# Edge attention: the quotient on another engine, the finish at another place, and twice the scatter buffers

## The chip, the cores and the metric

One core of a Trainium2 chip. The metric is the device time of one execution in microseconds (us). The kernel before took 1922.77 us, the median of three runs (1921.35 to 1923.86).

## The reference, cut to what matters

Two graph layers act on x (50,000 nodes of 64 channels) with 25,000 edges sorted by dst. The first is a pair of spline convolutions with a maximum over the edges of each target. The second, which the change is mostly about, is an attention whose softmax runs over the edges of each target node, channel by channel:

```python
d = gelu(layer_norm(gelu(layer_norm(coords @ Wd1 + bd1)) @ Wd2 + bd2))
logits = w1[target] - w2[source] + d
e = exp(logits - segment_max(logits, target)[target])
denom = segment_sum(e, target)
a = e / denom[target]
out = segment_sum(a * (w3[source] + d), target)
x = x + out
```

Here w1, w2 and w3 are products of relu(layer_norm(x)) with three 64x64 weights.

## The kernel before, in words

All edges are cut into 49 groups (`G`) of 512 (`EG`), four tiles (`TPG`) of 128. Five stages follow one another: preparation and the coordinate network's first part (to about 155 us), convolution 1 (to about 670 us), the network's second part and convolution 2 (to about 1280 us), a last norm and gelu of the network, and the attention (from about 1310 us).

Each engine has its own instruction stream, written out by hand as a function `step(g)` that the helper `each` (L322) calls for every group, four groups to a loop round. The order inside `step` is the order on the engine. Between engines there are only semaphores: `wait(eng, steps, g, name)` waits until the named step of group g is done, and `wait_fill` until a buffer of several has been filled by its DMA. Where a buffer has two copies it is chosen by `g.parity`, where it has four by `g.slot(SLOTS)`.

The attention of group g, with 64 channels of q and k logits and of values stacked in 128 partitions:

- GpSimd (POOL, L637 to L652) gathers the edge sources of group g+3 from `M2` (four indirect DMAs, L584), then scatters the finished rows of group g-1 into the output (four indirect DMAs, L591). The gather needs `gidx` of ScalarE (L828). The scatter needs `sidx` of ScalarE (L855) and the row of VectorE (L1592).
- SyncE loads the running maxima (L536), the cuts between targets (L539) and the base rows `b2` (L546) some groups ahead.
- VectorE (DVE): `normalise` (L1542) makes XT; `x1_ends` (L1532, L1535) adds gathered and loaded rows of group g+1 into `x1`; `running_max` (L1551, and a scan, L1554); `above_held` (L1561); `hold_full` (a scan for group g+2, L1523); `weigh_values` (L1568); `running_sums` (a scan, L1575). For group g-1, `reciprocal` (L1584) inverts the denominators and `finish` multiplies (L1589) and adds the node's own row into `srow` (L1592).
- ScalarE (ACT, L851 to L883): copies indices (L855, L828), copies the turned rows of group g+1 out of PSUM (L860), takes four activations for the two exponentials of group g (L866 to L871), squares (L876), and forms the inverse root of the variance of group g+1 by Ln and Exp (L881, L883).
- TensorE (PE): the q and v products of group g (L1085, two matmuls' worth of passes each), the turn of `x1` of g+1 (L1095), the offsets from d (L1078), the centring (L1099), the variance (L1104), a turn of the maxima of g+2 (L1111), and the turn of the sums of g (L1119) into bank 6, where `output` reads denominators and numerators.

The order of VectorE in the attention is this (L1596):

```python
if (g - 1).within(G): reciprocal(g - 1)
if now:               normalise(g)
if (g - 1).within(G): finish(g - 1)
if (g + 1).within(G): x1_ends(g + 1)
if now:               running_max(g); above_held(g)
if (g + 2).within(G): hold_full(g + 2)
if now:               weigh_values(g); running_sums(g)
```

`srow` and `sidx` (rows and indices to be scattered) have two copies, as have `x1` and the semaphores `scattered`. Convolution 1 scatters through the same two buffers into `T1` (its own `sidx` L765, `srow` L767 and L807); convolution 2 uses `srow` for rows that SyncE stores.

Of the kernel before, what the change touches and what calls it, by code (L numbers as in the profile page):

```python
# [31 lines left out]
P = 128  # L32
# [85 lines left out]
def build(nc, a, out):  # L118
# [17 lines left out]
    with ExitStack() as ctx:  # L136
# [6 lines left out]
        def pair(name):  # L143
            return [sem(name + "_even"), sem(name + "_odd")]
# [128 lines left out]
        full = [att_mem.take([C, EG]) for _ in (0, 1)]  # L273
        XR, rstd = (att_mem.take([P, EG]) for _ in (0, 1))
        pp, d0, rise = (att_mem.take([P, EG]) for _ in range(3))
        held = [att_mem.take([P, EG + 1]) for _ in (0, 1)]
        sums = [att_mem.take([P, EG]) for _ in (0, 1)]
        rec = att_mem.take([P, TPG, C])
        XT = [att_mem.take([P, EG]) for _ in (0, 1)]
        mx3 = [att_mem.take([P, MT * C]) for _ in (0, 1)]  # L280
        squares = lnq.rearrange("p t c -> p (t c)")


# [14 lines left out]

        bank = [ctx.enter_context(nc.psum_tensor(f"bank{i}", [P, 512], F32)) for i in range(8)]


        s_mem = sem("memsets")
        s_rows = sem("rows_loaded")
# [55 lines left out]
        def conv_sems(n):  # L359
            s = {  # L360
                "nload": pair(f"c{n}_nload"), "nstore": pair(f"c{n}_nstore"), "cut": pair(f"c{n}_cut"),
                "z": steps(f"c{n}_z", "z0 z1 z2 z3"), "turn": steps(f"c{n}_turn", "t0 t1 t2 t3"), "prod": steps(f"c{n}_prod", "m0 m1 m2 m3"),
                "zt": steps(f"c{n}_zt", "zt0 zt1 zt2 zt3"), "comb": steps(f"c{n}_comb", "v0 v1 v2 v3 pair quad msg"),
                "npe": steps(f"c{n}_npe", "nt nr"), "out": steps(f"c{n}_out", "out" if n == 1 else "acc out"),
                **signals(f"c{n}", "mt agg at row xn nts"),
            }
            if n == 1:
                s.update(signals("c1", "gidx sidx rowid esum ecen esq evar nsum ncen nsq nvar root a0r"))
                s["gathered"], s["scattered"] = pair("c1_gathered"), pair("c1_scattered")
# [11 lines left out]
        at = {  # L381
            "gathered": [sem(f"a_gathered_{i}") for i in range(SLOTS)], "scattered": pair("a_scattered"),
            "x1": steps("a_x1", "src dst"), "rstd": steps("a_rstd", "ln exp"),
            "bload": pair("a_bload"), "rload": pair("a_rload"), "cut": [sem(f"a_cut_{i}") for i in range(SLOTS)],
            "q": steps("a_q", "q1 q2"),
            "s1": steps("a_s1", "carry max rise"), "exp": steps("a_exp", "fall p gain d0"),
            "s2": steps("a_s2", "pv scan"), "fin": steps("a_fin", "rec y out"),
            **signals("a", "gidx sidx xt xr ce sq var xts rt full ft"),
        }

        def scatter_done(eng, s):

            for par in (0, 1):
                eng.wait_ge(s["scattered"][par], 16 * TPG * ((G + 1 - par) // 2))

        def stores_done(eng, sems, per=16):
            for par in (0, 1):
# [4 lines left out]
        def _(sp):  # L402
# [89 lines left out]
            def step2(g):  # L492
                if (g - 2).within(G):
                    n = g - 2
                    wait(sp, t["row"], n)
                    sp.sem_inc(sp_gate, 1)
                    sp.dma_start(M2[bass.ds(n.from_end(G, EG, 1), EG)].rearrange("(t p) c -> p t c", p=P),
                                 srow[n.parity][:, :, 0:C]).then_inc(t["mstore"][n.parity], 16)
# [54 lines left out]
        def _(pool):  # L553
# [35 lines left out]
            def scatter(g, s, table, bound, width):  # L589
                for j in range(TPG):  # L590
                    pool.indirect_dma_start(  # L591
                        out=table,
                        out_offset=bass.IndirectOffsetOnAxis(sidx[g.parity][:, j:j + 1], 0),
                        in_=srow[g.parity][:, j, 0:width], in_offset=None, bounds_check=bound, oob_is_err=False,
                    ).then_inc(s["scattered"][g.parity], 16)

            s = cs[1]

# [58 lines left out]
        def _(act):  # L657
# [88 lines left out]
            def conv(n):  # L746
                s = cs[n]

                def step(g):
# [11 lines left out]
                        gidx2(g + 3)  # L761
                    if n == 1 and (g - 1).within(G):
                        e = g - 1
                        wait_fill(act, s["scattered"], e - 2, 16 * TPG)
                        act.activation(sidx[e.parity][:, :], back_tiles_of(thirdI, e), ACT.Copy)\  # L765
                            .then_inc(s["sidx"].sem, 1)
                        act.activation(srow[e.parity][:, :, C], back_tiles_of(rowI, e), ACT.Copy)\  # L767
# [34 lines left out]
                    if (g - 1).within(G):  # L802
                        e = g - 1
                        wait(act, s["at"], e)
                        if n == 2:
                            wait_fill(act, s["mstore"], e - 2, 16)
                        act.activation(srow[e.parity][:, :, 0:C],  # L807
                                       bank[5][:, 0:TPG * C].rearrange("p (t c) -> p t c", c=C), ACT.Copy)\
                            .then_inc(s["row"].sem, 1)

# [78 lines left out]
        def _(pe):  # L889
# [191 lines left out]
            def step(g):  # L1081
# [6 lines left out]
                if (g + 1).within(G):  # L1088
# [4 lines left out]
                    rows = x1[e.parity].rearrange("p (t e) c -> p t (e c)", e=2)  # L1093
# [33 lines left out]
        def _(dve):  # L1127
            V_ = nc.vector

            V_.memset(pad16[:, :], 0.0)  # L1130
            V_.memset(srow[0][:, :, C:U], 0.0)
            V_.memset(srow[1][:, :, C:U], 0.0)
# [393 lines left out]
            def x1_ends(g):  # L1526

                wait_fill(dve, at["gathered"], g, 16 * TPG)
                wait_fill(dve, at["bload"], g, 16)
                X = x1[g.parity].rearrange("p (t e) c -> p t e c", e=2)  # L1530
# [47 lines left out]
            output = bank[6][:, :].rearrange("p (t h c) -> p t h c", h=2, c=C)  # L1578

            def reciprocal(g):  # L1580

                wait(dve, at["rt"], g)
                wait(dve, fin, g - 1, "out")
                V_.reciprocal(rec[:, :, :], output[:, :, 0, :]).then_inc(fin.sem, 1)  # L1584

            def finish(g):

                wait(dve, fin, g, "rec")
                V_.tensor_tensor(rec[:, :, :], rec[:, :, :], output[:, :, 1, :], ALU.mult).then_inc(fin.sem, 1)  # L1589
                wait(dve, fin, g, "y")  # L1590
                wait_fill(dve, at["scattered"], g - 2, 16 * TPG)
                V_.tensor_tensor(srow[g.parity][:, :, 0:C], rec[:, :, :],  # L1592
                                 x1[g.parity].rearrange("p (t e) c -> p t e c", e=2)[:, :, 0, :], ALU.add)\
# [47 lines left out]
```

## Time and profile before

| | us |
|---|---|
| median of 3 runs | 1922.77 |
| the profiled execution, its own time | 1922.7 |
| its span, first to last instruction | 1920.9 |
| VectorE busy in the span | 1560.4 (81%) |
| TensorE busy in the span | 1583.3 (82%) |
| GpSimd busy in the span | 1209.6 (63%) |
| ScalarE busy in the span | 697.3 (36%) |
| mean granted TensorE clock | 0.937 of full speed |

PE stands for TensorE, PEld for its weight loads, DVE for VectorE, ACT for ScalarE, POOL for GpSimd, SP for SyncE. A row of the timeline has the start, the duration, the engine, the line of the kernel, the operation, what it writes and reads, and in brackets how long its engine had been idle before it and what ended that. On POOL a short pause between two DMAs, in which nothing is waited for, stands as "issue". The shares over the whole span are averages over unlike stages, so what the attention stage is bound by is read in the stage.

### The profile page before, as it was taken

To read this page: it belongs to the slowest core of one execution; us is meant where nothing else is said; L and a number is where in the kernel's file an instruction comes from. 1 tells how busy PE (TensorE), PEld (TensorE's weight loads), DVE (VectorE), ACT (ScalarE), POOL (GpSimd) and SP (SyncE) were. 2 spreads that over 40 slices of the span, in tenths; PEclk is the share of its full clock that TensorE was granted. 3 is DMA by queue.
4 is the path that set the end of the run, shared out by engine and by line. 5 is a ranking of instruction groups with operands and counts; after the bars stand their busy time and mean duration, and the time that the engine had idled before them with its cause. 6 is when DMAs were issued, how large, how long until landed. Compare 5 with 4: busy or idle time off the path is not lost.

```text
span 1920.9 us, 33986 instructions
## 1 busy us (share of the span) xinstructions
PE 1583.3 (82%) x7745; PEld 1024.9 (53%) x7745; DVE 1560.4 (81%) x2878; ACT 697.3 (36%) x1743; POOL 1209.6 (63%) x1207
## 2 busy tenths in 40 slices
PE   1987898989899869999999999977777777777774
PEld 1254566656666656777777777754433334334342
DVE  2588899999999958899889899867777777777775
ACT  1463333333333332333323223235333444444432
POOL 4004777777777757777767767514666666666664
PEclk9998999999999989999999999989888888888887
DMA  8942444444444436877777777732323222323220
GB/s 136 164 55 61 96 106 104 103 102 103 106 103 105 95 100 181 233 225 229 232 218 232 230 220 226 225 84 57 64 63 63 63 63 63 64 62 63 63 57 12
DMA packets 408085, 232.10 MB, mean 121 GB/s; under 512 B 305989, under 2 KB 381958, under 8 KB 408046
## 3 DMA queue, kind: packets, MB, share of 16 engines
q1 hardware_dynamic: 312158, 152.47, 29.8%
q0 software_dynamic: 44864, 65.52, 15.3%
q10 hardware_dynamic: 51024, 13.68, 5.6%
q8 instruction: 14, 0.23, 0.0%
q14 instruction: 25, 0.20, 0.0%
HBM read 141.71 MB, written 92.64 MB: 122 GB/s over the span
## 4 chain that ended last, share of the span: by engine, by line
PE 39%; issue 9%; ACT 7%; DVE 7%; POOL 1%; DMA 1%; DVEq 0%; ACTq 0%; SPq 0%; POOLq 0%
PE bank L964 16%; PE bank L1085 5%; PE bank L1104 3%; PE bank L957 3%; PE bank L1006 2%; PE bank L1023 2%; DVE arena L1554 2%; ACT arena L869 2%; PE bank L995 1%; ACT lnq L876 1%; DVE arena L1542 1%; ACT arena L866 1%; PE bank L1015 1%; PE bank L984 1%; PE bank L1032 1%
## 5 line engine op out<-in xcount | busy, mean ns | idle before, releaser
L964 PE MATMUL bank<-Wk,arena 128*128 128x320 f32 (+1 forms) x2352 | 655.6, 464 | 56.7 <-ACT arena L755 56.7
L964 PEld LDWEIGHTS bank<-Wk,arena 128*128 128x128 f32 (+1 forms) x2352 | 327.3, 189 | 303.1 <-issue 221.7
L584 POOL DMA_INDIRECT gath<-T,gidx x392 | 385.8, 984 | 149.3 <-issue 113.0
L584 POOL DMA_INDIRECT gath<-M,gidx x196 | 196.2, 1001 | 206.3 <-ACT gidx L828 107.9
L584 POOL DMA_INDIRECT gath<-in_x_dram,gidx x196 | 197.5, 1008 | 189.3 <-ACT gidx L673 130.8
L755 ACT ACTIVATE arena<-bank 128x256 f32<-128x256 f32 (+1 forms) x392 | 169.3, 432 | 308.2 <-PE bank L957 307.6
L591 POOL DMA_INDIRECT T<-srow,sidx x196 | 216.1, 1103 | 80.4 <-issue 58.7
L591 POOL DMA_INDIRECT out_dram<-srow,sidx x196 | 198.3, 1012 | 75.7 <-issue 59.7
L1332 DVE TENSOR_TENSOR arena<-bank,A 128x320 f32<-128x320 f32 x392 | 191.5, 489 | 66.1 <-PE bank L964 58.7
L957 PE MATMUL bank<-ident,arena 128*128 128x128 f32 x980 | 171.6, 274 | 13.1 <-DVE arena L1312 13.1
L1085 PE MATMUL bank<-arena,Wqk 128*128 128x512 f32 x98 | 79.1, 900 | 117.8 <-DVE arena L1542 117.8
L957 PEld LDWEIGHTS bank<-ident,arena 128*128 128x128 f32 x980 | 124.4, 142 | 44.1 <-issue 7.3
L1584 DVE RECIPROCAL arena<-bank 128x256 f32<-128x256 f32 x49 | 86.1, 1758 | 73.5 <-PE bank L1119 73.5
L860 ACT ACTIVATE arena<-bank 128x512 f32<-128x512 f32 x49 | 29.3, 597 | 276.9 <-PE bank L1095 276.9
L1324 DVE TENSOR_TENSOR_SCAN arena<-ends_cut,arena,bank 64x512 f32<-64x512 bf16 x98 | 123.9, 1264 | 0.3 <-PE bank L984 0.3
L1078 PE MATMUL bank<-DT,spread 128*128 (+1 forms) x392 | 118.1, 431 | 0.0
L1006 PE MATMUL bank<-rootpair,nhT 128*128 128x128 f32 x784 | 103.6, 275 | 0.0
L1078 PEld LDWEIGHTS bank<-DT,spread 128*128 128x128 f32 x392 | 84.4, 228 | 31.9 <-issue 23.4
L1006 PEld LDWEIGHTS bank<-rootpair,nhT 128*128 128x128 f32 x784 | 95.4, 192 | 0.3
L1312 DVE TENSOR_TENSOR arena<-lnc,a0r 128x320 f32<-128x320 f32 x196 | 93.7, 480 | 0.0
L1104 PE MATMUL bank<-lnq,means 128*128 128x512 f32 x98 | 53.7, 630 | 42.7 <-ACT lnq L876 42.7
L1085 PEld LDWEIGHTS bank<-arena,Wqk 128*128 128x128 f32 x98 | 19.7, 251 | 129.3 <-DVE arena L1542 129.3
(185 smaller groups left out, 2800.8 us busy)
## 6 DMA issues: line engine op xcount, KB each, us to landing
arena<-T SPq DMA_DIRECT2D x48, 816.0 KB
T<-arena SPq DMA_DIRECT2D x96, 272.0 KB
T<-zero ACTq DMA_DIRECT2D x1, 13281.2 KB, 103.8
B<-arena SPq DMA_DIRECT2D x49, 256.0 KB
arena<-B SPq DMA_DIRECT2D x49, 256.0 KB, 3.6
arena<-in_x_dram SPq DMA_DIRECT2D x48, 256.0 KB, 4.1
out_dram<-arena SPq DMA_DIRECT2D x48, 256.0 KB
begins_cut<-begins_d SPq DMA_DIRECT2D x49, 128.5 KB, 3.4
```

The costliest lines, as they stand in the source:

```text
L584: pool.indirect_dma_start(out=gath[slot][:, j, k, 0:width], out_offset=None, in_=table, in_offset=bass.IndirectOffsetOnAxis(gidx[slot][:, ...
L591: pool.indirect_dma_start(out=table, out_offset=bass.IndirectOffsetOnAxis(sidx[g.parity][:, j:j + 1], 0), in_=srow[g.parity][:, j, 0:width ...
L755: act.activation(ZT[j // 2][:, first:first + chunks, :], bank[j % 2][:, 0:chunks * P], ACT.Relu)\
L957: tr = pe.transpose(bank[j % 2][:, c * P:c * P + P], Z[g.parity][:, j // 2, (first + c) * P:(first + c + 1) * P], ident[:, :])
L964: return pe.matmul(bank[2 + r][:, 0:KO], ZT[q][rows, chunk, :], Wk[n - 1][rows, weights].rearrange("p k o -> p (k o)"), start=start, stop= ...
L1006: mm = pe.matmul(bank[7][:, q * P:q * P + P], nhT[:, q * P:q * P + P], root[n - 1][:, :], start=True, stop=True)
L1078: pe.matmul(bank[b + e.parity].rearrange("p (t h e) -> p h t e", h=2, e=P)[:, j], spread[:, j, :], pairs, start=(j == 0), stop=False, skip ...
L1085: pe.matmul(bank[b + g.parity][:, :], W[:, :, :].rearrange("p t c -> p (t c)"), XT[g.parity][:, :], start=False, stop=True, skip_group_che ...
L1104: pe.matmul(bank[7][:, :], means[:, :], squares, start=True, stop=True).then_inc(at["var"].sem, 1)
L1312: V_.tensor_tensor(Z[g.parity][:, j // 2, at_:at_ + KO].rearrange("p (k c) -> p k c", c=C), row.broadcast_to([P, K, C]), w.unsqueeze(2).br ...
L1324: V_.tensor_tensor_scan(agg[g.parity][:, ::-1], ends_cut[g.parity][:, ::-1], bank[4][0:C, ::-1], agg[1 - g.parity][:, 0:1], ALU.add, ALU.max)\
L1332: V_.tensor_tensor(V[:, j].rearrange("p (k o) -> p k o", o=C), bank[2 + j % 2][:, 0:KO].rearrange("p (k o) -> p k o", o=C), A1[:, bass.ds( ...
```

## The change

Four things are done together:

1. The quotient. `reciprocal` on VectorE goes. In its place ScalarE takes Ln of the denominators in bank 6 and then Exp with scale -1 of that, right after the copy of `sidx` and ahead of the copy of the turned rows. `rec` has two copies.
2. The order on VectorE. `finish(g - 1)` moves from behind `normalise(g)` to behind `above_held(g)`, ahead of `hold_full(g + 2)` and of the value product.
3. `sidx`, `srow` and the semaphores `scattered` have four copies instead of two, in the attention and in convolution 1. ScalarE and VectorE wait for the scatter of four groups ago and no longer for that of two groups ago.
4. `x1` has four copies, so that `x1_ends(g + 1)` waits for the finish of group g-3 and not of g-1. Buffers in the shared region `arena` lie in another order, and two more small memsets run at the start.

```diff
-        sidx = [sb(f"sidx{i}", [P, TPG], I32) for i in (0, 1)]
-        srow = [sb(f"srow{i}", [P, TPG, U]) for i in (0, 1)]
+        sidx = [sb(f"sidx{i}", [P, TPG], I32) for i in range(SLOTS)]
+        srow = [sb(f"srow{i}", [P, TPG, U]) for i in range(SLOTS)]
...
-        x1 = [att_mem.take([P, 2 * TPG, C]) for _ in (0, 1)]
+        x1 = [att_mem.take([P, 2 * TPG, C]) for _ in range(SLOTS)]
...
 # ScalarE, attention
-                    wait_fill(act, at["scattered"], e - 2, 16 * TPG)
-                    act.activation(sidx[e.parity][:, :], tiles_of(outI, e), ACT.Copy).then_inc(at["sidx"].sem, 1)
+                    wait_fill(act, at["scattered"], e - SLOTS, 16 * TPG)
+                    act.activation(sidx[e.slot(SLOTS)][:, :], tiles_of(outI, e), ACT.Copy).then_inc(at["sidx"].sem, 1)
+                if (g - 1).within(G):
+                    e = g - 1
+                    wait(act, at["rt"], e)
+                    wait(act, at["fin"], e - 2, "out")
+                    act.activation(rec[e.parity][:, :, :], output[:, :, 0, :], ACT.Ln).then_inc(at["rec"].sem, 1)
+                    wait(act, at["rec"], e, "ln")
+                    act.activation(rec[e.parity][:, :, :], rec[e.parity][:, :, :], ACT.Exp, scale=-1.0)\
+                        .then_inc(at["rec"].sem, 1)
...
 # VectorE, attention
-                wait(dve, fin, g - 2, "out")
+                wait(dve, fin, g - SLOTS, "out")
...
-            def reciprocal(g):
-
-                wait(dve, at["rt"], g)
-                wait(dve, fin, g - 1, "out")
-                V_.reciprocal(rec[:, :, :], output[:, :, 0, :]).then_inc(fin.sem, 1)
...
             def finish(g):
 
-                wait(dve, fin, g, "rec")
-                V_.tensor_tensor(rec[:, :, :], rec[:, :, :], output[:, :, 1, :], ALU.mult).then_inc(fin.sem, 1)
+                wait(dve, at["rec"], g, "exp")
+                r = rec[g.parity]
+                V_.tensor_tensor(r[:, :, :], r[:, :, :], output[:, :, 1, :], ALU.mult).then_inc(fin.sem, 1)
                 wait(dve, fin, g, "y")
-                wait_fill(dve, at["scattered"], g - 2, 16 * TPG)
+                wait_fill(dve, at["scattered"], g - SLOTS, 16 * TPG)
...
-                if (g - 1).within(G):
-                    reciprocal(g - 1)
                 if now:
                     normalise(g)
-                if (g - 1).within(G):
-                    finish(g - 1)
                 if (g + 1).within(G):
                     x1_ends(g + 1)
                 if now:
                     running_max(g)
                     above_held(g)
+                if (g - 1).within(G):
+                    finish(g - 1)
                 if (g + 2).within(G):
                     hold_full(g + 2)
                 if now:
                     weigh_values(g)
                     running_sums(g)
```

## Rows read from the trace of the kernel before

**Rows 1.** Windows: stretch, length, busy PE, PEld, DVE, ACT, POOL, clock, DMA.

```profile
240.00:640.00 400.00, 357.26 (x1994) 244.90 (x1992) 382.60 (x886) 146.65 (x440) 309.95 (x295) 1.00 0.49 104
1350.00:1850.00 500.00, 367.02 (x1148) 199.58 (x1148) 367.53 (x491) 200.28 (x410) 324.42 (x327) 0.84 0.28 62
```

**Rows 2.** Line L1542, normalise: durations min, median, max, first and last start.

```profile
L1542 DVE SCALAR_TENSOR_TENSOR arena<-bank,arena x49: 627/628/691, 1314.9 to 1898.3; 128x512 f32<-128x512 f32 x49
```

**Rows 3.** Timeline of one group of the attention, ACT, DVE and PE.

```profile
1604.06 0.69 ACT L881 ACTIVATE arena<-bank,eps_col 128x512 f32<-128x512 f32 x1 [1.37 <-PE bank L1104]
...
1604.78 0.63 ACT L883 ACTIVATE arena<-arena 128x512 f32<-128x512 f32 x1
1605.04 1.76 DVE L1584 RECIPROCAL arena<-bank 128x256 f32<-128x256 f32 x1 [1.44 <-PE bank L1119]
...
1606.72 0.63 DVE L1542 SCALAR_TENSOR_TENSOR arena<-bank,arena 128x512 f32<-128x512 f32 x1
...
1607.40 2.08 PE L1085 MATMUL bank<-arena,Wqk 128*128 128x512 f32 x2 [2.40 <-DVE arena L1542]
...
1609.52 1.28 DVE L1554 TENSOR_TENSOR_SCAN arena<-bank,arena,begins_cut 128x512 f32<-128x512 f32 x1 [0.53 <-PE bank L1085]
...
1610.92 0.69 DVE L1561 TENSOR_TENSOR arena<-bank,arena 128x512 f32<-128x512 f32 x1
...
1611.43 0.60 ACT L860 ACTIVATE arena<-bank 128x512 f32<-128x512 f32 x1 [5.93 <-PE bank L1095]
1611.53 1.27 DVE L1523 TENSOR_TENSOR_SCAN arena<-begins_cut,arena 64x512 f32<-64x512 bf16 x1
...
1612.02 0.62 ACT L866 ACTIVATE arena<-arena 128x512 f32<-128x512 f32 x1
...
1614.52 1.28 DVE L1575 TENSOR_TENSOR_SCAN arena<-arena 128x512 f32<-128x512 f32 x1 [0.49 <-ACT arena L871]
...
1615.21 1.10 PE L1104 MATMUL bank<-lnq,means 128*128 128x512 f32 x2 [1.14 <-ACT lnq L876]
...
1619.00 0.63 DVE L1542 SCALAR_TENSOR_TENSOR arena<-bank,arena 128x512 f32<-128x512 f32 x1
```

**Rows 4.** Waits between 1400 and 1800 us: total, times, longest.

```profile
ACT arena L860 <- PE bank L1095: 192.7, 33, 6.8
...
POOL gath L584 <- ACT gidx L828: 67.7, 31, 3.0
```

**Rows 5.** Timeline of that group, POOL: a scatter, the first gather, the next scatter.

```profile
1609.84 0.98 POOL L591 DMA_INDIRECT out_dram<-srow,sidx  x1 [0.30 <-issue]
...
1613.05 0.99 POOL L584 DMA_INDIRECT gath<-M,gidx  x1 [2.23 <-ACT gidx L828]
...
1618.11 1.03 POOL L591 DMA_INDIRECT out_dram<-srow,sidx  x1 [0.30 <-issue]
```

**Rows 6.** Groups by line and form, 1350 to 1850 us.

```profile
L591 POOL DMA_INDIRECT out_dram<-srow,sidx x163 | 165.4, 1015 | 49.7 <-issue 49.7
L584 POOL DMA_INDIRECT gath<-M,gidx x164 | 159.2, 971 | 126.1 <-ACT gidx L828 85.7 <-issue 40.5
...
L1592 DVE TENSOR_TENSOR srow<-arena 128x256 f32<-128x256 f32 x41 | 17.4, 425 | 3.4
```

**Rows 7.** Timeline: a gather that starts inside a VectorE scan, in the attention.

```profile
1342.22 1.27 DVE L1523 TENSOR_TENSOR_SCAN arena<-begins_cut,arena 64x512 f32<-64x512 bf16 x1
...
1342.59 1.69 POOL L584 DMA_INDIRECT gath<-M,gidx  x1 [0.54 <-issue]
```

**Rows 8.** Timeline: a scatter that starts inside a VectorE product, in convolution 1.

```profile
402.53 0.68 DVE L1360 TENSOR_TENSOR arena<-arena,jst 128x512 f32<-128x512 f32 x1
...
402.71 1.40 POOL L591 DMA_INDIRECT T<-srow,sidx  x1 [0.32 <-issue]
```

**Rows 9.** Windows of 1 us, PE alone: length, busy, granted clock, DMA.

```profile
1608.00:1609.00 1.00, 1.00 (x2) 0.50 0.08 26
...
1612.00:1613.00 1.00, 1.00 (x4) 1.00 0.00 0
```

More of the change, by code:

```diff
@@ L269, in build @@
         att_mem = Arena()
-        x1 = [att_mem.take([P, 2 * TPG, C]) for _ in (0, 1)]
+        x1 = [att_mem.take([P, 2 * TPG, C]) for _ in range(SLOTS)]
         b2 = [att_mem.take([P, TPG, 2 * C]) for _ in (0, 1)]
         runs = [att_mem.take([C, EG]) for _ in (0, 1)]
-        full = [att_mem.take([C, EG]) for _ in (0, 1)]
         XR, rstd = (att_mem.take([P, EG]) for _ in (0, 1))
         pp, d0, rise = (att_mem.take([P, EG]) for _ in range(3))
+        full = [att_mem.take([C, EG]) for _ in (0, 1)]
         held = [att_mem.take([P, EG + 1]) for _ in (0, 1)]
         sums = [att_mem.take([P, EG]) for _ in (0, 1)]
-        rec = att_mem.take([P, TPG, C])
+        rec = [att_mem.take([P, TPG, C])]
         XT = [att_mem.take([P, EG]) for _ in (0, 1)]
         mx3 = [att_mem.take([P, MT * C]) for _ in (0, 1)]
+        rec.append(att_mem.take([P, TPG, C]))
         squares = lnq.rearrange("p t c -> p (t c)")
@@ L299, in build @@
         bank = [ctx.enter_context(nc.psum_tensor(f"bank{i}", [P, 512], F32)) for i in range(8)]
+        output = bank[6][:, :].rearrange("p (t h c) -> p t h c", h=2, c=C)
         s_mem = sem("memsets")
@@ L368, in conv_sems @@
                 s.update(signals("c1", "gidx sidx rowid esum ecen esq evar nsum ncen nsq nvar root a0r"))
-                s["gathered"], s["scattered"] = pair("c1_gathered"), pair("c1_scattered")
+                s["gathered"], s["scattered"] = pair("c1_gathered"), [sem(f"c1_scattered_{i}") for i in range(SLOTS)]
                 s["xstore"] = pair("c1_xstore")
@@ L381, in build @@
         at = {
-            "gathered": [sem(f"a_gathered_{i}") for i in range(SLOTS)], "scattered": pair("a_scattered"),
+            "gathered": [sem(f"a_gathered_{i}") for i in range(SLOTS)], "scattered": [sem(f"a_scattered_{i}") for i in range(SLOTS)],
             "x1": steps("a_x1", "src dst"), "rstd": steps("a_rstd", "ln exp"),
@@ L386, in build @@
             "s1": steps("a_s1", "carry max rise"), "exp": steps("a_exp", "fall p gain d0"),
-            "s2": steps("a_s2", "pv scan"), "fin": steps("a_fin", "rec y out"),
+            "s2": steps("a_s2", "pv scan"), "rec": steps("a_rec", "ln exp"), "fin": steps("a_fin", "y out"),
             **signals("a", "gidx sidx xt xr ce sq var xts rt full ft"),
@@ L391, in scatter_done @@
         def scatter_done(eng, s):
-            for par in (0, 1):
-                eng.wait_ge(s["scattered"][par], 16 * TPG * ((G + 1 - par) // 2))
+            for slot in range(SLOTS):
+                eng.wait_ge(s["scattered"][slot], 16 * TPG * ((G + SLOTS - 1 - slot) // SLOTS))
         def stores_done(eng, sems, per=16):
@@ L497, in step2 @@
                     sp.dma_start(M2[bass.ds(n.from_end(G, EG, 1), EG)].rearrange("(t p) c -> p t c", p=P),
-                                 srow[n.parity][:, :, 0:C]).then_inc(t["mstore"][n.parity], 16)
+                                 srow[n.slot(SLOTS)][:, :, 0:C]).then_inc(t["mstore"][n.parity], 16)
                 if (g - 1).within(G):
@@ L592, in scatter @@
                         out=table,
-                        out_offset=bass.IndirectOffsetOnAxis(sidx[g.parity][:, j:j + 1], 0),
-                        in_=srow[g.parity][:, j, 0:width], in_offset=None, bounds_check=bound, oob_is_err=False,
-                    ).then_inc(s["scattered"][g.parity], 16)
+                        out_offset=bass.IndirectOffsetOnAxis(sidx[g.slot(SLOTS)][:, j:j + 1], 0),
+                        in_=srow[g.slot(SLOTS)][:, j, 0:width], in_offset=None, bounds_check=bound, oob_is_err=False,
+                    ).then_inc(s["scattered"][g.slot(SLOTS)], 16)
             s = cs[1]
@@ L763, in step @@
                         e = g - 1
-                        wait_fill(act, s["scattered"], e - 2, 16 * TPG)
-                        act.activation(sidx[e.parity][:, :], back_tiles_of(thirdI, e), ACT.Copy)\
+                        wait_fill(act, s["scattered"], e - SLOTS, 16 * TPG)
+                        act.activation(sidx[e.slot(SLOTS)][:, :], back_tiles_of(thirdI, e), ACT.Copy)\
                             .then_inc(s["sidx"].sem, 1)
-                        act.activation(srow[e.parity][:, :, C], back_tiles_of(rowI, e), ACT.Copy)\
+                        act.activation(srow[e.slot(SLOTS)][:, :, C], back_tiles_of(rowI, e), ACT.Copy)\
                             .then_inc(s["rowid"].sem, 1)
@@ L806, in step @@
                             wait_fill(act, s["mstore"], e - 2, 16)
-                        act.activation(srow[e.parity][:, :, 0:C],
+                        act.activation(srow[e.slot(SLOTS)][:, :, 0:C],
                                        bank[5][:, 0:TPG * C].rearrange("p (t c) -> p t c", c=C), ACT.Copy)\
@@ L1092, in step @@
                     pe.sem_inc(pe_gate, 1)
-                    rows = x1[e.parity].rearrange("p (t e) c -> p t (e c)", e=2)
+                    rows = x1[e.slot(SLOTS)].rearrange("p (t e) c -> p t (e c)", e=2)
                     for j in range(TPG):
@@ L1130, in _ @@
             V_.memset(pad16[:, :], 0.0)
-            V_.memset(srow[0][:, :, C:U], 0.0)
-            V_.memset(srow[1][:, :, C:U], 0.0)
+            for t in srow:
+                V_.memset(t[:, :, C:U], 0.0)
             V_.memset(rows_i[:, 0], 0).then_inc(s_mem, 1)
@@ L1576, in running_sums @@
                                       ALU.mult, ALU.add).then_inc(s2.sem, 1)
[L1578 to L1584 removed]
             def finish(g):
[L1588 to L1589 removed]
+                wait(dve, at["rec"], g, "exp")
+                r = rec[g.parity]
+                V_.tensor_tensor(r[:, :, :], r[:, :, :], output[:, :, 1, :], ALU.mult).then_inc(fin.sem, 1)
                 wait(dve, fin, g, "y")
[L1591 to L1593 removed]
+                wait_fill(dve, at["scattered"], g - SLOTS, 16 * TPG)
+                V_.tensor_tensor(srow[g.slot(SLOTS)][:, :, 0:C], r[:, :, :],
+                                 x1[g.slot(SLOTS)].rearrange("p (t e) c -> p t e c", e=2)[:, :, 0, :], ALU.add)\
                     .then_inc(fin.sem, 1)
```

2 lines of the change are left out of this document (1 added, 1 removed).

## The prediction, as it was put on record

> **What bounds the kernel now.** I first read the windows by stage, since the shares over the whole span mix stages [rows 1]. Convolution 1 has VectorE busy for 382.60 of 400 us at full clock. In the attention no engine is full: VectorE 367.53 of 500 us, TensorE 367.02 at a mean clock of 0.84, GpSimd 324.42. Such a stage is bound by a chain that goes round the engines once a group. Its pace is in the starts of normalise: 1314.9 to 1898.3 us for 49 of them [rows 2], so 583.4 / 48 = 12.15 us a group, and 583 us in all.
>
> Next I read the timeline of one group for what released what [rows 3]. Normalise (1606.72) releases the q product (1607.40), that the scan of maxima (1609.52), that the difference (1610.92). ScalarE meanwhile waits for the turned rows and copies them (1611.43), then starts the exponentials (1612.02). These end in the squares, the variance product on TensorE (1615.21), Ln and Exp on ScalarE, and the next normalise (1619.00). One link doesn't belong to this chain of data. The Exp of the preceding group ended at 1604.78 + 0.63 = 1605.41, and normalise, which needs only that, started at 1606.72, because the reciprocal (1605.04, 1.76 us) stood ahead of it in VectorE's queue. Normalise therefore comes some 1.28 us later than its data, allowing 0.03 us for the semaphore.
>
> The waits say who has room [rows 4]. ScalarE waits 192.7 us for the turned rows in 33 groups, 5.8 us each. GpSimd waits 67.7 us for its indices in 31 groups, 2.2 us each. GpSimd's room is the smaller one, and the forecast turns on it.
>
> **The quotient.** It removes 49 reciprocals of 1.76 us from VectorE and with them the 1.28 us a group on the chain. It adds a Ln and an Exp over 256 elements to ScalarE. The trace shows these two functions at 512 elements, 0.69 and 0.63 us [rows 3], so the pair costs between nothing and 1.32 us; I take 1.0, nearer the upper end, as a half-size activation keeps its fixed part. It stands where ScalarE now idles for 5.93 us ahead of its copy of the turned rows [rows 3]. The sums' turn in bank 6 is there by 1605.04, before ScalarE is through with the Exp (1605.41), so the Ln waits for nothing. I cost it at nothing; without that cover it would be 1.0 us a group. By itself the step makes a group 12.15 - 1.28 = 10.87 us.
>
> **The finish behind the difference.** Its two instructions (0.41 and 0.42 us, [rows 6] for the second) leave the stretch between normalise and the scan of maxima. In the group shown the scan waited for the q product anyway (0.53 us), so nothing is won there; in groups with a quick q product the scan could start up to 0.9 us sooner. But ScalarE's exponentials sit behind its copy of the turned rows (1611.43 to 1612.02), which comes later than the difference ends (1611.61), so I count nothing. The same 0.87 us now stand ahead of hold_full and the value product. Hold_full ended at 1612.80 and the sums' scan waited for ScalarE till 1614.52, so they fit within about 0.1 us. The scatter's row comes some 3 us later after normalise than now. GpSimd reaches its scatters only at 1618.11 [rows 5], so this too is hidden.
>
> **Buffers.** No row shows VectorE or ScalarE waiting for a scatter, neither in the attention nor in convolution 1, so four copies of `srow`, `sidx` and `x1` bring nothing by themselves. They let GpSimd fall further behind before anyone feels it. The queues of SyncE and GpSimd keep their DMAs. The two memsets write 16 columns each, less than a measurement can tell. Convolution 1 and 2 I leave as they are, between 2 us faster and 2 us slower.
>
> **The clock.** The q product took 2.08 us while the granted clock was 0.50 (the 1.2 GHz level), after TensorE had been idle for 2.40 us; by 1612 the clock was at 1.00 [rows 3, 9]. With the reciprocal gone that idle time is about 1.1 us. The clock may fall less often, which is worth from nothing to 1.0 us a group (half of the 2.08). I take half, 0.5 us: the chain alone would then run at about 10.4 us a group.
>
> **GpSimd, late next.** Per group it issues four gathers and four scatters [rows 6]: 4 x 0.971 + 4 x 1.015 + 8 x 0.30 of issue = 10.34 us. At 12.15 us a group it idles; at 10.4 it has nothing left. And its DMAs do not always take that long. A gather that starts at 1342.59 inside hold_full's scan (1342.22 to 1343.49) takes 1.69 us instead of 0.97: it ends 0.79 us after the scan [rows 7]. In convolution 1 a scatter that starts inside a product takes 1.40 us instead of 1.02 and ends 0.90 us after it [rows 8]. All these VectorE instructions have both inputs in SBUF. The scan of maxima, which reads a bank, does no such thing: the scatter that starts at 1609.84 inside it takes 0.98 us [rows 3, 5]. So each VectorE instruction with two SBUF inputs can hold a starting DMA until its end. The DMA is through 0.8 us after that, and takes 0.97 on its own, so the last 0.2 us cost nothing: at most 1.27 - 0.2 = 1.07 us are lost for hold_full and as much for the scan of sums, and at most 0.2 us for each of two additions. That is 0 to 2.6 us a group.
>
> Now these hold-ups are nearly absent because the burst is timed by `gidx`: the gather starts at 1613.05, just after hold_full (1612.80) [rows 3, 5]. The change moves hold_full 0.87 us later against the index copy, onto the gather's start. Once GpSimd lags, its burst also slides along VectorE's work. A start comes every 1.3 us and each scan lasts 1.28, so about one start falls into each at any point of it: half of 1.07, twice, is 1.07 us. GpSimd then needs 10.34 + 1.07 = 11.4 us a group.
>
> The Trainium skill bears on this. The page "SBUF — State Buffer", section "Who interferes with whom", says that a VectorE instruction with two SBUF inputs contends with a GpSimd instruction that reads SBUF, and the trace agrees by the 1.69 us. It also infers that tensor_tensor leaves descriptor generation alone; the scatter of 1.40 us speaks against that. By the inference the hold-up would be nothing and the sum would be the second rival's.
>
> **The sum.** At first the chain sets the pace, since gathers run ahead of their use. The four that start at 1613.05 are issued by 1618 and read by x1_ends two groups on, at 1607.4 + 2 x 10.4 = 1628; less 2 us for the landing, my estimate, GpSimd may lose 8 us before anyone waits. At 1.0 us lost a group that lasts 8 groups: 8 x (12.15 - 10.4) = 14 us. The other 40 run at GpSimd's pace: 40 x (12.15 - 11.4) = 30 us. At the end the last quotient takes 1.0 us instead of 1.76: 0.7 us. Together 45 us against the profiled execution's own time of 1922.7 (span 1920.9 and 1.8 around it), which is 0.1 us from the median: 1878 us.
>
> **Rivals.** *First, GpSimd keeps up.* Its burst locks to the scans so that the hold-ups only fill its idle time, and the clock pattern stays. The chain goes at 10.87: 48 x 1.28 + 0.7 = 62 us, so 1861 us. For it speaks convolution 1, where such long scatters stand beside a VectorE that is 96% busy; against it, that there is only 0.5 us of room here. Chance 0.22.
>
> *Second, no hold-ups to speak of.* GpSimd runs at 10.34 and the chain at 10.4: 48 x 1.75 + 0.7 = 85 us, so 1838 us. Against it speak the long DMAs. Chance 0.10.
>
> *Third, slower.* The hold-up is near its upper bound: GpSimd at 10.34 + 2.6 = 12.94 us for 40 groups loses 40 x 0.79 = 32 us, against 14 + 1 won before: 17 us slower, 1939 us. It decides from a hold-up of 2.2 us a group, where 40 x (12.5 - 12.15) eats the 15. For it: after being held, the next DMA starts 1.1 us behind the scan's end, where the scan of sums may have begun. Against it: every start would have to fall on a scan's beginning. Chance 0.05.
>
> *Fourth, little moved.* GpSimd at 11.9 to 12.2 us a group leaves 1903 to 1922 us, with hold-ups of 1.6 to 1.9 us. Chance 0.05. Were the change not to take the reciprocal off the path at all, the time would be that of now; I count it here.
>
> **How the numbers follow.** The forecast, GpSimd as the bound with partial hold-ups, has 0.58 and a range of its own of 1862 to 1902 us (hold-ups of 0.7 to 1.6 us, 40 x 0.5 us about the middle, with the clock's term). 1838 and 1861 lie below, so the range goes from 1836 to 1902; it leaves out the slower case, the fourth, and part of the second. A measurement of this kernel tells apart about 0.2%, 3.8 us. Slower has 0.05, same 0.02 (from the fourth), faster the other 0.93.
>
> **What would show it.** Right: the L584 row of the attention has a mean over 1.1 us and "issue" as the only thing GpSimd waits for; normalise starts 11.3 us apart on average but 10.4 or so in the first eight groups; VectorE or TensorE idles for a DMA ahead of L1532. First rival: GpSimd still waits for gidx now and then, pace 10.9. Second: DMAs at 0.97 and 1.02 us, pace 10.4. ScalarE's Ln and Exp should show about 0.5 us each, with no idle time before them; normalise should start within 0.05 us of the Exp's end. It would be wrong if the Ln waited for the sums' turn, or the clock stayed low through the stage.

## The result, and the profile after

The changed kernel takes 1869.95 us (median of four runs, 1865.1 to 1873.23), against 1922.34 us for the kernel before (also four runs). The ratio is 0.9723, with a 95% interval of 0.9705 to 0.974. The forecast was 1878 us in a range of 1836 to 1902.

The page of the changed kernel, in its parts on busy time, on the chain that ended last, and on groups by line:

```profile
PE 1540.2 (82%) x7745; PEld 997.7 (53%) x7745; DVE 1481.6 (79%) x2831; ACT 736.9 (39%) x1841; POOL 1253.6 (67%) x1207
...
PE 30%; POOL 19%; issue 10%; DMA 2%; DVE 2%; ACT 1%; POOLq 0%; DVEq 0%; SPq 0%; ACTq 0%
...
L587 POOL DMA_INDIRECT gath<-M,gidx x196 | 238.3, 1216 | 122.4 <-issue 58.5
...
L594 POOL DMA_INDIRECT out_dram<-srow,sidx x196 | 200.9, 1025 | 61.2 <-issue 60.9
```

VectorE has 79 us less to do, the 49 reciprocals of 1.76 us less 7 us by which other lines grew; ScalarE has 40 us more. GpSimd has the same 1207 instructions and is busy 44 us longer, nearly all of it in the attention's gathers: they take 1.216 us each and took 1.0. A fifth of the chain that ended last now runs through GpSimd (19%, for 1% before).

The windows by stage, with the columns of [rows 1]: convolution 1, the attention, and the attention's first eight groups and its rest:

```profile
240.00:640.00 400.00, 356.99 (x1986) 244.17 (x1984) 382.42 (x884) 146.98 (x443) 309.57 (x296) 1.00 0.48 104
1350.00:1800.00 450.00, 322.23 (x1130) 171.30 (x1130) 296.89 (x441) 228.94 (x482) 353.57 (x317) 0.92 0.32 68
...
1313.70:1392.00 78.30, 57.53 (x224) 31.38 (x224) 57.76 (x87) 44.76 (x94) 50.52 (x45) 1.00 0.32 68
1392.00:1845.50 453.50, 324.67 (x1116) 171.90 (x1116) 295.16 (x440) 227.50 (x480) 355.99 (x321) 0.91 0.30 65
```

Convolution 1 is as it was [rows 1]: 382.42 us of VectorE for 382.60. The attention's clock rose from 0.84 to 0.92.

Normalise in the changed kernel, as a line and as two rows of the timeline, its first and its ninth:

```profile
L1553 DVE SCALAR_TENSOR_TENSOR arena<-bank,arena x49: 691/692/693, 1313.7 to 1845.5; 128x512 f32<-128x512 f32 x49
...
1313.70 0.69 DVE L1553 SCALAR_TENSOR_TENSOR arena<-bank,arena 128x512 f32<-128x512 f32 x1 [4.70 <-ACT arena L894]
...
1392.00 0.69 DVE L1553 SCALAR_TENSOR_TENSOR arena<-bank,arena 128x512 f32<-128x512 f32 x1 [1.61 <-ACT arena L894]
```

From the first to the last it is 531.8 us, 11.08 a group; before it was 583.4 [rows 2]. So 51.6 of the 53.3 us between the two spans (1920.9 and 1867.6) lie there. The stage starts 1.2 us sooner, and the end behind the last normalise is 22.1 instead of 22.6 us. The pace has two parts: eight groups at (1392.0 - 1313.7) / 8 = 9.8 us, then forty at (1845.5 - 1392.0) / 40 = 11.3 us.

One of the later groups in the timeline, to be laid beside [rows 3]:

```profile
1604.87 0.63 ACT L894 ACTIVATE arena<-arena 128x512 f32<-128x512 f32 x1
...
1605.55 0.39 ACT L863 ACTIVATE arena<-bank 128x256 f32<-128x256 f32 x1
1605.62 0.69 DVE L1553 SCALAR_TENSOR_TENSOR arena<-bank,arena 128x512 f32<-128x512 f32 x1 [1.75 <-ACT arena L894]
1605.97 0.42 ACT L865 ACTIVATE arena<-arena 128x256 f32<-128x256 f32 x1
...
1606.37 1.12 PE L1096 MATMUL bank<-arena,Wqk 128*128 128x512 f32 x2 [1.28 <-DVE arena L1553]
...
1609.06 0.42 DVE L1543 TENSOR_TENSOR arena<-gath,arena 128x256 f32<-128x256 f32 x1 [2.75 <-DMA gath<-M,gidx]
...
1610.71 0.60 ACT L871 ACTIVATE arena<-bank 128x512 f32<-128x512 f32 x1 [4.32 <-PE bank L1106]
...
1615.01 1.28 DVE L1586 TENSOR_TENSOR_SCAN arena<-arena 128x512 f32<-128x512 f32 x1 [0.21 <-DVE arena L1579]
...
1615.29 1.76 POOL L587 DMA_INDIRECT gath<-M,gidx  x1 [0.31 <-issue]
```

The Exp of the variance ends at 1605.50 and normalise starts at 1605.62, with nothing ahead of it. Ln and Exp of the quotient take 0.39 and 0.42 us, and ScalarE still waits 4.32 us afterwards. The stall that is new stands before L1543: VectorE waits 2.75 us for a gather to land. And one of the gathers starts 0.28 us into the scan of sums and takes 1.76 us, to 0.76 us after that scan's end.

The waits of the changed kernel between 1400 and 1800 us:

```profile
ACT arena L871 <- PE bank L1106: 123.1, 35, 4.7
...
DVE arena L1543 <- DMA gath<-M,gidx: 55.3, 34, 2.7
...
POOL out_dram L594 <- issue: 42.7, 140, 0.3
POOL gath L587 <- issue: 42.7, 140, 0.3
...
POOL gath L587 <- ACT gidx L831: 0.6, 2, 0.3
```

GpSimd's wait for its indices is down from 67.7 us [rows 4] to 0.6. It issues one DMA after the other, and VectorE waits for what lands.

### The profile page after: what moved, and what is told of

Same layout as the page of the kernel before. It is cut to its first block, busy times and chain, and to the rows that moved or that the text cites. A ratio compares the mean times of both kernels' runs of the same rounds, so it can differ in the third digit from the quotient of the medians.

```text
span 1867.6 us, 34016 instructions
## 1 busy us (share of the span) xinstructions
PE 1540.2 (82%) x7745; PEld 997.7 (53%) x7745; DVE 1481.6 (79%) x2831; ACT 736.9 (39%) x1841; POOL 1253.6 (67%) x1207
## 4 chain that ended last, share of the span: by engine, by line
PE 30%; POOL 19%; issue 10%; DMA 2%; DVE 2%; ACT 1%; POOLq 0%; DVEq 0%; SPq 0%; ACTq 0%
PE bank L975 17%; POOL gath L587 10%; POOL out_dram L594 8%; PE bank L968 3%; PE bank L1017 2%; PE bank L1034 2%; PE bank L1006 1%; PE bank L995 1%; PE bank L1026 1%; PE bank L1043 1%; DMA arena<-T 1%; DMA gath<-M,gidx 1%; PE bank L935 1%; DVE arena L1227 0%; DMA T<-arena 0%
## 5 line engine op out<-in xcount | busy, mean ns | idle before, releaser
L587 POOL DMA_INDIRECT gath<-M,gidx x196 | 238.3, 1216 | 122.4 <-issue 58.5
L1096 PE MATMUL bank<-arena,Wqk 128*128 128x512 f32 x98 | 66.5, 766 | 54.6 <-DVE arena L1553 54.6
L1553 DVE SCALAR_TENSOR_TENSOR arena<-bank,arena 128x512 f32<-128x512 f32 x49 | 33.9, 692 | 87.5 <-ACT arena L894 87.5
L1089 PE MATMUL bank<-DT,spread 128*128 (+1 forms) x392 | 103.2, 386 | 0.0
L871 ACT ACTIVATE arena<-bank 128x512 f32<-128x512 f32 x49 | 29.3, 597 | 161.5 <-PE bank L1106 161.5
L775 ACT ACTIVATE arena<-bank 128x512 f32<-128x512 f32 x49 | 29.3, 598 | 154.5 <-PE bank L1026 154.5
L1089 PEld LDWEIGHTS bank<-DT,spread 128*128 128x128 f32 x392 | 73.4, 198 | 29.1 <-issue 23.4
```

The lines of the kernel that those rows point to most:

```text
L587: pool.indirect_dma_start(out=gath[slot][:, j, k, 0:width], out_offset=None, in_=table, in_offset=bass.IndirectOffsetOnAxis(gidx[slot][:, ...
L1089: pe.matmul(bank[b + e.parity].rearrange("p (t h e) -> p h t e", h=2, e=P)[:, j], spread[:, j, :], pairs, start=(j == 0), stop=False, skip ...
L1096: pe.matmul(bank[b + g.parity][:, :], W[:, :, :].rearrange("p t c -> p (t c)"), XT[g.parity][:, :], start=False, stop=True, skip_group_che ...
```

## The experiments

**e1: the buffers alone.** The changed kernel with the reciprocal and finish as before, so that only the four copies of `x1`, `srow` and `sidx` are left (`rec` keeps its two).

```diff
-                    act.activation(rec[e.parity][:, :, :], output[:, :, 0, :], ACT.Ln).then_inc(at["rec"].sem, 1)
...
+                V_.reciprocal(rec[g.parity][:, :, :], output[:, :, 0, :]).then_inc(fin.sem, 1)
...
+                if (g - 1).within(G):
+                    reciprocal(g - 1)
                 if now:
                     normalise(g)
+                if (g - 1).within(G):
+                    finish(g - 1)
...
-                if (g - 1).within(G):
-                    finish(g - 1)
```

> The kernel before with the four copies of x1, srow and sidx alone; reciprocal and finish as before. Theory (the reciprocal on the path, then GpSimd as the bound): nobody waited for a scatter, so 1918 to 1926 us, and GpSimd still waits for gidx some 2 us a group. Rival (two scatter buffers held the stage back): 1905 us or less.

1923.95 us, ratio 1.0002 (0.9987 to 1.0017). GpSimd waits 64.1 us for its indices between 1400 and 1780. Without the quotient's move, the buffers bring nothing.

**e2: the quotient alone.** Ln and Exp on ScalarE in the kernel before; finish stays behind normalise, and there are two buffers.

```diff
+                    act.activation(rec[e.parity][:, :, :], output[:, :, 0, :], ACT.Ln).then_inc(at["rec"].sem, 1)
...
-                if (g - 1).within(G):
-                    reciprocal(g - 1)
                 if now:
                     normalise(g)
...
```

> The kernel before with Ln and Exp on ScalarE alone; finish behind normalise, two buffers. Theory: the reciprocal's 1.28 us a group leaves the chain and GpSimd becomes the bound near 11.1 us a group, 1868 to 1885 us, GpSimd waiting for issue alone. Rival (the place of finish is what counts, since finish now waits behind normalise for ScalarE's Exp and holds x1_ends and the scan up by about 1 us): 1895 us or more, GpSimd still waiting for gidx.

1867.76 us, ratio 0.9704 (0.9673 to 0.9735), which the changed kernel's ratio can't be told from. This one edit (with a second copy of `rec`) carries the whole gain, and the rival's time of 1895 us or more did not come. Two of its waits, 1400 to 1800 us, and GpSimd's two groups from 1350 to 1800 us:

```profile
DVE arena L1551 <- ACT arena L892: 70.4, 37, 2.1
...
POOL gath L585 <- ACT gidx L829: 12.0, 7, 1.9
```

```profile
L585 POOL DMA_INDIRECT gath<-M,gidx x164 | 174.7, 1065 | 61.9 <-issue 48.2 <-ACT gidx L829 13.7
L592 POOL DMA_INDIRECT out_dram<-srow,sidx x163 | 163.6, 1004 | 49.7 <-issue 41.4 <-ACT gidx L829 8.2
```

It gets there in another way: normalise goes at 527.0 / 48 = 10.98 us a group, the gathers are stretched less (1.065 us), and GpSimd now and then does wait for its indices, which I had not expected. This is my first rival's picture: in this kernel VectorE never waits for a gather to land, and the chain sets the pace. What makes its chain longer than the 9.8 us of the changed kernel's first groups is the place of finish. One group of the changed kernel, from its first eight, and one of e2:

```profile
1362.40 0.69 DVE L1553 SCALAR_TENSOR_TENSOR arena<-bank,arena 128x512 f32<-128x512 f32 x1 [1.64 <-ACT arena L894]
1363.14 1.12 PE L1096 MATMUL bank<-arena,Wqk 128*128 128x512 f32 x2 [1.19 <-DVE arena L1553]
1364.31 1.28 DVE L1565 TENSOR_TENSOR_SCAN arena<-bank,arena,begins_cut 128x512 f32<-128x512 f32 x1 [0.49 <-PE bank L1096]
```

```profile
1523.96 0.69 DVE L1551 SCALAR_TENSOR_TENSOR arena<-bank,arena 128x512 f32<-128x512 f32 x1 [2.01 <-ACT arena L892]
1524.70 1.13 PE L1094 MATMUL bank<-arena,Wqk 128*128 128x512 f32 x2 [1.27 <-DVE arena L1551]
1526.80 1.28 DVE L1563 TENSOR_TENSOR_SCAN arena<-bank,arena,begins_cut 128x512 f32<-128x512 f32 x1
```

The q product is equally quick in both, but the scan of maxima starts 1.91 us after normalise in the one and 2.84 us after it in the other, where the two instructions of finish stand between. Most groups of e2 last 10.8 us. So the changed kernel and e2 take the same time under two different bounds: there GpSimd, but for the first eight groups (11.08 us a group over all), here the chain (10.98).

**e3: two scatter buffers in the changed kernel.** `srow`, `sidx` and the semaphores `scattered` back to two.

```diff
-                    wait_fill(act, at["scattered"], e - SLOTS, 16 * TPG)
+                    wait_fill(act, at["scattered"], e - 2, 16 * TPG)
...
```

> The changed kernel with two copies of srow and sidx again. Theory: GpSimd issues without a pause in either case, so the pace a group stays near 11.1 us; only the delay that GpSimd may run up at the start is about one group less, up to 8 us in all: 1868 to 1880 us. Rival (four buffers carry part of the gain, as ScalarE's copy of sidx now waits for the scatter of two groups ago and with it everything behind it): 1890 us or more.

1878.03 us, ratio 0.9755 (0.9724 to 0.9786). The wait that the four buffers remove, 1400 to 1800 us:

```profile
ACT sidx L858 <- DMA out_dram<-srow,sidx: 148.6, 35, 4.5
```

ScalarE stands 4.2 us a group ahead of the copy of `sidx`, and the whole costs only some 8 us by the medians, less than the two intervals' width can settle. Of the 11.6 us by which its profiled execution is longer than the changed kernel's, 6.1 lie ahead of the attention, which starts at 1319.8 us (in e4, with its four buffers, at 1320.5), and 5.9 in it. GpSimd stays almost without a pause, so a wait of 4 us elsewhere hardly matters.

**e4: the reciprocal on VectorE, but late.** The changed kernel with the reciprocal between the difference and finish.

```diff
+                if (g - 1).within(G):
+                    reciprocal(g - 1)
                 if (g - 1).within(G):
                     finish(g - 1)
```

> The changed kernel with the reciprocal back on VectorE, but right ahead of finish, behind the difference. Theory: what cost time was the place ahead of normalise, not the engine; VectorE has room (353 of 532 us busy) and GpSimd stays the bound: 1865 to 1882 us. Rival (the 1.76 us must leave VectorE, since the value product and the scan of sums come 1.8 us later and the sums' turn with them): 1895 us or more, with VectorE or TensorE waiting instead of GpSimd's DMAs.

1881.76 us, ratio 0.977 (0.9729 to 0.9812): four fifths of the gain, with the reciprocal's 1.76 us still on VectorE. So most of what it cost was its place ahead of normalise, and the rival (1895 us or more) fails. Of the 14.8 us between the two profiled executions 6.8 lie ahead of the attention, where nothing differs, and 5.4 in its first eight groups (10.46 us each, for 9.8). The forty groups behind them go at 11.37 us, as in the changed kernel (11.34). So the later place costs time only until GpSimd is the bound. TensorE has a new wait, for the scan of sums ahead of the sums' turn, but it stands mostly where GpSimd sets the pace:

```profile
PE bank L1122 <- DVE arena L1578: 40.4, 35, 1.5
```

**e5 to e7, times that can't be used.** The three kernels of e8 to e10 were first measured where the kernel before itself took 2349.64 us, not 1922. They took 2441.73, 2400.49 and 2292.33 us: none lies in its expected range, and the first two are slower than the kernel before. What made all four slow, and these two more so, stays open.

> The changed kernel, but ScalarE writes the gain (the last of its four exponentials) into bank 2 or 3 instead of SBUF, so that the scan of sums has one input in SBUF instead of two. Theory (a VectorE instruction with two SBUF inputs holds up a starting indirect DMA): no DMA is stretched by the scan of sums any more, the mean gather falls from 1.21 to about 1.1 us, GpSimd's group from 11.1 to about 10.7 us, 1850 to 1862 us. Rival (the long gathers come from queues or memory, whatever VectorE reads): 1866 to 1874 us and gathers of 1.7 us still beside the scan of sums.

> The kernel of e5, and hold_full reads bank 7 in place of the loaded maxima, so that neither scan has two SBUF inputs (this leaves the true running maxima out of the computation; TensorE's variance product now waits for that scan). Theory: gathers and scatters of 0.97 and 1.02 us nearly everywhere, GpSimd 10.4 us a group, the chain about the same: 1836 to 1848 us. Rival (queues or memory): 1866 to 1874 us.

> The changed kernel with three of the four scatters of a group in the attention (a quarter of the rows is not written). Theory (GpSimd is the bound): 1.3 us less on GpSimd a group, the chain takes over at 10.4 to 10.9 us: 1840 to 1860 us, and GpSimd waits for gidx again. Rival (the chain of the other engines is the bound at 11.1 us already): 1866 to 1874 us.

The durations of single DMAs can be read even there. In e6 the last 176 of the attention's gathers took 0.962 us on average and not one over 1.05 us; the same 176 in e7, where the scans are as in the changed kernel, took 1.159 us. Whatever slowed those executions did not lengthen the gathers of e6, so the stretching goes with the scans' inputs.

**e8: the gain into a bank.** The changed kernel; the scan of sums reads the gain from bank 2 or 3 and thus has one input in SBUF. All results are computed as before.

```diff
-                    act.activation(d0[:, :], d0[:, :], ACT.Exp, scale=-1.0).then_inc(at["exp"].sem, 1)
+                    act.activation(bank[2 + g.parity][:, :], d0[:, :], ACT.Exp, scale=-1.0).then_inc(at["exp"].sem, 1)
...
-                    offsets(e, 2, "s1", "rise")
+                    offsets(e, 2, "s2", "scan")
...
-                V_.tensor_tensor_scan(sums[g.parity][:, :], d0[:, :], pp[:, :], sums[1 - g.parity][:, EG - 1:EG],
+                V_.tensor_tensor_scan(sums[g.parity][:, :], bank[2 + g.parity][:, :], pp[:, :], sums[1 - g.parity][:, EG - 1:EG],
```

> The kernel of e5 on a chip where the kernel before takes about 1922 us (in the call of e5 it took 2350). Theory: no DMA is stretched by the scan of sums, which now costs GpSimd 0.74 us a group; GpSimd's group falls from 11.3 to about 10.6 us once it is late, 1845 to 1856 us. Rival (queues or memory): 1866 to 1874 us.

1850.67 us, ratio 0.9619 (0.9591 to 0.9646), faster than both kernels. Two pairs of its timeline, a gather that starts inside the scan of sums and one inside hold_full's scan:

```profile
1500.09 1.28 DVE L1586 TENSOR_TENSOR_SCAN arena<-bank,arena 128x512 f32<-128x512 f32 x1 [0.19 <-DVE arena L1579]
1500.26 0.94 POOL L587 DMA_INDIRECT gath<-M,gidx  x1 [0.31 <-issue]
...
1508.61 1.27 DVE L1534 TENSOR_TENSOR_SCAN arena<-begins_cut,arena 64x512 f32<-64x512 bf16 x1
1509.26 1.40 POOL L587 DMA_INDIRECT gath<-M,gidx  x1 [0.30 <-issue]
```

The first starts 0.17 us into a scan of 1.28 us and takes 0.94 us, where its like in the changed kernel took 1.76. The second, beside the scan that still has two inputs in SBUF, takes 1.40. Over the attention the scan of sums now holds nothing up; hold_full's scan holds up more than it did, 0.49 us a group for 0.20.

**e9: neither scan with two inputs in SBUF.** As e8, and hold_full reads bank 7 (the true running maxima are left out). TensorE's variance product, which writes that bank, now waits for hold_full's scan.

```diff
-                V_.tensor_tensor_scan(full[g.parity][:, :], begins_cut[g.slot(SLOTS)][0:C, 0:EG], runs[g.parity][:, :],
+                V_.tensor_tensor_scan(full[g.parity][:, :], begins_cut[g.slot(SLOTS)][0:C, 0:EG], bank[7][0:C, :],
...
```

> The kernel of e6 again, same reason (hold_full reads a bank instead of the true maxima). Theory: GpSimd back to back at 10.3 to 10.4 us a group, 1836 to 1846 us. Rival (queues or memory): 1866 to 1874 us.

1829.19 us, ratio 0.952 (0.9493 to 0.9548), 7 us below what was expected. GpSimd's two groups, 1350 to 1800 us:

```profile
L594 POOL DMA_INDIRECT out_dram<-srow,sidx x178 | 178.1, 1001 | 54.2 <-issue 50.6 <-ACT gidx L831 3.7
L587 POOL DMA_INDIRECT gath<-M,gidx x172 | 166.1, 966 | 52.4 <-issue 51.8 <-ACT gidx L831 0.3 <-ACT sidx L858 0.3
```

The gathers are back at 0.966 us and the scatters at 1.001. GpSimd still has almost no pause: 4 x 0.966 + 4 x 1.001 + 8 x 0.305 = 10.3 us, which is the distance of its gathers. Normalise goes at 488.0 / 48 = 10.17 us, nearly every group at 10.1, and VectorE never waits for a gather. So here the chain sets the pace, a little longer than 9.8 us (the variance product starts 0.48 us behind the squares, for 0.23 in the changed kernel's first groups), and GpSimd falls behind so slowly that the stage ends before anyone feels it.

**e10: three scatters of four.** The changed kernel, and a quarter of the attention's rows is not written.

```diff
-                    scatter(n, at, out, out_bound, C)
+                    scatter(n, at, out, out_bound, C, 3)
```

> The kernel of e7 again, same reason (three of four scatters in the attention). Theory: the chain of the other engines becomes the bound, whose pace the first eight groups of the changed kernel show, 9.6 to 9.9 us; with GpSimd at 9.0 plus 0.7 of hold-ups, 1800 to 1830 us. Rival (the chain is the bound at 11.1 us already): 1866 to 1874 us.

1821.92 us, ratio 0.9476 (0.9448 to 0.9504), 48 us less than the changed kernel by the ratios. Normalise goes at 479.9 / 48 = 10.0 us with gathers of 1.184 us, most groups at 9.8 us, and VectorE never waits for a gather. Less work for GpSimd, with all of the other engines' work in place, brings this: GpSimd was the bound. (The left-out rows' transfers go too; in e9 all transfers are there, and the wait for gathers has gone as well.)

**e11: e8 with finish early.**

```diff
                 if now:
                     normalise(g)
+                if (g - 1).within(G):
+                    finish(g - 1)
...
-                if (g - 1).within(G):
-                    finish(g - 1)
```

> The kernel of e8 with finish back behind normalise, as e2 had it. Theory (finish's place moves hold_full against GpSimd's starts and does little else): within 6 us of e8, either way. Rival (finish ahead of x1_ends waits for ScalarE and lengthens the chain, which shows now that GpSimd has less to do): 6 us or more slower than e8.

1862.54 us, ratio 0.9683 (0.9635 to 0.9731), 12 us slower than e8 by the medians; the two intervals overlap a little. The rival is favoured: GpSimd again waits 14.0 us for its indices between 1400 and 1780, and undisturbed groups last 10.5 to 10.6 us, for 9.8 in e8. It is what e2 shows: the early finish lengthens the chain, and it costs time where GpSimd is not slower still.

## Why the prediction was right

**The quotient** went as forecast: the chain alone, seen in the first eight groups, goes at 9.8 us a group; Ln and Exp cost 0.39 + 0.42 us where I had taken 1.0, in time that ScalarE had free. By e2 this edit alone is the gain, by e4 most of it is the place of the reciprocal and not its engine.

**The clock and the finish.** I took half a microsecond a group for the clock, nothing for the finish, and a chain of 10.4 us. In the first eight groups the clock was at 1.00 all along and the chain took 9.8 us. That is 8 x 0.6 = 5 us. The clock alone does not explain it, as e2 shows: its q product is as quick (1.13 us), but finish stands ahead of the scan of maxima, and most of its groups last 10.8. The prediction had said that "in groups with a quick q product the scan could start up to 0.9 us sooner" and then counted nothing for it; that is the mis-sized term. The 1.1 us between 10.87 and 9.8 need both, a quick q product and nothing between it and the scan; no run separates them further. Once VectorE waits for gathers, the idle times are back and the clock is at 0.91.

**GpSimd, late next,** was the step on which the forecast stood, and it held. It issues without a pause; the mean gather is 1.216 us; VectorE waits for the gather's landing ahead of L1543; the first eight groups are quick and the others go at 11.3 us, for 11.4 forecast. Over all DMAs of the attention that start inside a VectorE instruction and end late, what they take beyond 0.97 us (a gather) or 1.015 us (a scatter) is 0.74 us a group by the scan of sums, 0.20 by hold_full and 0.06 by the two additions (L1543 and L1597), 1.00 us in all where I took 1.07; and 10.34 + 1.00 is the 11.34 measured. The split was not even, though: I had let one start fall "into each at any point of it". In fact the starts are locked to the scans: 44 of the 49 that fall into the scan of sums do so in its first half microsecond, most of them 0.15 to 0.35 us in, and many of those in hold_full's scan fall near its end. That the two errors cancel is luck. e8 takes the 0.74 away, hold_full's share grows to 0.49, and 40 x (1.00 - 0.52) = 19 us is what it wins; e9 wins another 21. That the quick groups are eight is in part luck too: the gathers' landing, which I took as 2 us, is 3.4 us from the issue in the view of DMAs.

**The buffers** were put at nothing. e1 confirms that without the quotient; e3 shows the scatter buffers worth at most some 8 us with it, not clear of the noise. The finish was put at nothing too, and the total agrees (e2 and the changed kernel can't be told apart), but for another reason than mine: what it saves on the chain is lost again, because GpSimd is then the bound.

**The sum.** 1878 was forecast and 1870 measured. The difference is 5 us of the quick groups, 40 x 0.06 = 2 us of GpSimd's pace, and 1.2 us by which the stage began sooner. That last one is chance: though hardly anything ahead of it differs, the attention starts anywhere between 1313.7 and 1320.5 us in the changed kernel, the kernel before, e1 to e4 and e8 to e11.

**The rivals.** The first (GpSimd keeps up, 10.87 us) did not come for this change but nearly describes e2. The second (no hold-ups) is e9, made by hand: 1829 us where I had given 1838 us. It needed the scans to be changed. The inference of the Trainium skill, page "SBUF — State Buffer", section "Who interferes with whom", that tensor_tensor does not stall descriptor generation, does not hold in these runs: in the changed kernel's attention 25 DMAs start inside one of the two additions, and the 18 of them that take longer end 0.82 to 0.90 us behind it. The sentence beside it, that a VectorE instruction with two SBUF inputs contends with a GpSimd instruction that reads SBUF, holds. The third and fourth needed hold-ups of 1.6 us a group or more; they were 1.00. The fourth's times were added up wrongly: by the sum's own terms 11.9 to 12.2 us a group give 1898 to 1910 us and not 1903 to 1922.

## What to carry to other kernels

When an instruction leaves the chain, ask which engine has the least room left, and count its issue time too: here it was one that stood at 65% busy. Indirect DMAs that GpSimd issues are stretched by VectorE instructions with both inputs in SBUF, so a busy share read at one pace is not what the engine needs at another, when its starts fall elsewhere. Moving one input of a long VectorE scan into a bank was worth 19 us here, without making the scan any shorter. And two versions that take the same time need not have the same bound: e2 and the changed kernel look alike until GpSimd is relieved.

## What the runs showed of the hardware

In the attention, an indirect DMA that starts while VectorE is in an instruction with two SBUF inputs ends 0.75 to 0.91 us after that instruction, whether the start fell 0.1 us or 0.9 us into it; one that starts in the last 0.2 us loses nothing. The same scan shows no such effect with one input in a bank (0.94 us, for 1.76 with its gain in SBUF).

The very beginning of the instruction is an exception. In all profiled executions, each DMA that starts up to 0.08 us into a scan with two inputs in SBUF takes 0.94 to 1.02 us (45 of them in the attention), and each that starts 0.09 to 0.2 us into one takes 1.83 to 1.99 (111 of them). One that was not held, in the changed kernel:

```profile
1432.05 1.33 DVE L1534 TENSOR_TENSOR_SCAN arena<-begins_cut,arena 64x512 f32<-64x512 bf16 x1
1432.13 0.97 POOL L587 DMA_INDIRECT gath<-M,gidx  x1 [0.30 <-issue]
```

Here the scan is the one that loses something: 1.33 us instead of 1.27. Every such scan with a DMA start 0.06 to 0.08 us into it takes 1.31 to 1.34 us, and no other takes over 1.30. So whichever of the two comes first keeps the other waiting.

Normalise takes 0.69 us where it comes after idle time, and took 0.63 where the reciprocal ran just before it [rows 2]. In e4, where nothing runs just before it, it takes 0.69 again.
